# Four blocks of a cross-attention kernel made one, its high parts taken straight from the exponent, and its output computed in 512-token units

## The chip, the cores and the metric

The kernel runs on one core of a Trainium2 chip. The metric is the device time of one execution in microseconds (us), the median of a few runs. A core has five engines that work side by side, each through its own list of instructions in order: TensorE (PE, matrix products into the accumulator memory PSUM; its weight loads are listed as PEld), VectorE (DVE), ScalarE (ACT), GpSimd (POOL) and SyncE (SP, which here only issues DMA transfers). They wait for one another through counting semaphores.

## The reference

Two batches of 1024 query tokens with 640 features attend to 2044 context tokens with 384 features, in 8 heads of 80 (`D`). The four context tokens behind those form a second, small attention: they ask over the residual, and the result asks four keys again. Both results are summed, multiplied by `Wout`, and bias and residual are added. Cut to what matters:

```
query = hidden_states @ Wq;  keyt = enc @ Wk;  valt = enc @ Wv      # enc: 2044 tokens
hs = mha(query, keyt, valt)                                         # 8 heads of 80
ca_q1 = einsum('btc,th->bch', ca, Wq_ca)[:, indices, :]             # ca: 4 tokens
ca_hs1 = mha(ca_q1, residual, residual)
ca_hs2 = mha(ca_hs1 @ Wq, ca @ Wk_ca, ca @ Wv_ca)
out = (hs + ca_hs2) @ Wout + b_out + residual
```

## The kernel before

All arithmetic is float32. TensorE runs the large products in its faster `fp32r` format, in which an operand has fewer bits, so each operand is split into a high part (the value rounded to `fp32r`) and a low part (value minus high part), and a product is three matmuls: high by high, high by low, low by high. ScalarE makes high parts, VectorE low parts.

The program is four blocks, one after another. At the end of a block (`with nc.Block()`) all engines meet at a barrier before any of them begins the next.

- **project** (0 to about 291 us). For both batches, 512 tokens at a time, it makes keys, values, queries and `u` (for the small attention) in a fixed list of `jobs`. Job n writes PSUM bank n % 8; ScalarE evicts the high part, VectorE the low part, and SP writes both to HBM. Interleaved "m" jobs find score maxima of the small attention. `ctx_f` holds two context chunks as they arrive. At the first job of chunk c ScalarE splits chunk c+1 (`split_ctx`, L403), also at the very first job of all.
- **tokens** (to about 456 us): the small attention, 16 heads of four steps. `scores` (L942), ACT's exponent (L770), products with the residual (L973); in between `fold_tokens` (L897) and `fold_keys` (L906) combine weights; `gather` (L926) and `low_gathered` (L839) make `p2g` at the end, `fold_values` (L917) makes `vw`. SP begins with `written`, a wait until all of project's writes have landed, then loads `wk2`, `wqT` (L717) and later the first head's keys. Before that, in project, eight small DMAs (`shift_tokens`, L633) put negated maxima in place; a head's scores wait for all eight.
- **attend** (to about 1178 us): the main attention, 16 heads (`G`) of 16 key tiles (`KT`), so 256 steps `n`. A step is: scores of tile n+2 (four matmuls, L1166) into one of two PSUM tiles `at_s_ps`; ACT's exponent of it to `probs` (L1107), and a second ACT pass over `probs` that makes the high part `prob_hi` (L1113); the low part `prob_lo` on VectorE (L1041), or for tiles 4, 9 and 14 of a head on GpSimd; and six matmuls of tile n's values (L1183). Two further matmuls per step (`score_piece`, L177) compute scores of the next head so that VectorE (L185) can take their maxima; the last head has no such pieces. The score PSUM tile is free after L1107. The values wait for the low part ahead of all six matmuls. After a head ACT takes the result (L1119), and SP, VectorE and GpSimd (L222) divide it by the sum and write it to `heads_d`.
- **output** (the rest): 16 tiles of 128 tokens. Each loads its `heads_d` piece (L1252), the residual (L1254) and a piece of `p2g` (L1255), splits it (ACT L1281, DVE L1304), runs 30 + 2 matmuls (L1335, L1339) into one of two PSUM tiles, adds residual and bias (L1318) and stores. The last head's division runs beside the first tiles.

A group of matmuls is paced by what its weights and moving operand cost and by the semaphores in front of it. What sets the order of the work around the change is only the order in which the code is written, engine by engine, and these waits.

## Time and profile before

| | |
|---|---|
| three runs | 1273.33, 1271.99, 1273.00 us; median 1273.0 |
| the profiled execution | 1273.22 us, its span 1271.4 us |
| PE busy | 1234.0 us, 97% of the span |
| DVE, ACT, POOL busy | 820.8 (65%), 721.3 (57%), 209.6 us (16%) |
| largest idle times in front of a matmul | 7.0 us (start of output), 5.2 (start of tokens), 4.4 (in project), 3.1 us (start of attend) |

The span is the time from the first to the last instruction of the profiled execution; the 1.8 us around it are not in the trace. The engines' shares are averages over stages with different limits. The ends of matmuls in the timeline are modelled and overlap the next start, so the pace of a run of matmuls is read from start to start. The granted clock of PE is given as a share of 2.4 GHz: 1.00 is 2.4 GHz, 0.50 is 1.2 GHz. In a timeline, what stands in brackets is the time for which the engine did nothing before the row, and what ended it.

### The profile page before, as it was taken

The numbers are of one execution on the slowest core, as the hardware profiler recorded it, in microseconds if no ns is written. First come the engines' busy times: TensorE is split into PE (matmuls) and PEld (weight loads), VectorE is DVE, ScalarE is ACT, GpSimd is POOL, SyncE is SP. The second block draws the span as 40 slices with busy tenths as digits, with TensorE's granted clock in tenths as the row PEclk, the third lists the DMA queues.
The fourth block names the chain that finished last, engine by engine and source line by source line (L and its number), as shares of the span: only waits on it lengthen the run. The fifth ranks groups of instructions, "written<-read, shape, count | busy, mean of one in ns | idle before, by whom it ended". The sixth has DMA issues, their size and how long they took to land. (4 is left out here: it accounts for less than half of the span.)

```text
span 1271.4 us, 15103 instructions
## 1 busy us (share of the span) xinstructions
PE 1234.0 (97%) x5652; PEld 968.8 (76%) x5652; DVE 820.8 (65%) x1147; ACT 721.3 (57%) x784; POOL 209.6 (16%) x112
## 2 busy tenths in 40 slices
PE   6999999998999989999999999999999999999798
PEld 5888988896667667777777777777777777776798
DVE  4448825681234368888888888888887887864223
ACT  5332424222444456777777777777777777778111
POOL 1100000000000011212212321221221222123232
PEclk9999999997999999999999999999999999999899
DMA  7995798896650052453254244335425424210566
GB/s 245 281 334 193 208 288 238 276 260 142 191 147 1 1 153 78 112 141 95 77 146 104 82 127 110 107 107 146 97 71 146 104 89 120 65 53 22 166 201 185
DMA packets 106686, 181.44 MB, mean 143 GB/s; under 512 B 18185, under 2 KB 62729, under 8 KB 102490
## 3 DMA queue, kind: packets, MB, share of 16 engines
q1 hardware_dynamic: 101194, 162.71, 46.7%
q0 software_dynamic: 2688, 11.80, 2.9%
q10 hardware_dynamic: 2736, 6.03, 1.3%
q8 instruction: 42, 0.69, 0.2%
q14 instruction: 26, 0.21, 0.1%
HBM read 116.32 MB, written 63.24 MB: 141 GB/s over the span
## 5 line engine op out<-in xcount | busy, mean ns | idle before, releaser
L185 DVE TENSOR_REDUCE mpart<-at_mx_ps 128x1 f32<-128x512 f32 x480 | 326.2, 685 | 108.5 <-PE at_mx_ps L177 106.4
L1107 ACT ACTIVATE probs<-at_s_ps 128x1024 f32<-128x1024 f32 (+1 forms) x256 | 262.7, 1026 | 158.1 <-PE at_s_ps L1166 158.1
L1041 DVE TENSOR_TENSOR prob_lo<-probs,prob_hi 128x1024 fp32r<-128x1024 f32 (+1 forms) x208 | 270.3, 1299 | 38.0 <-ACT prob_hi L1113 37.9
L1113 ACT ACTIVATE prob_hi<-probs 128x1024 fp32r<-128x1024 f32 (+1 forms) x256 | 271.4, 1060 | 7.6
L1041 POOL TENSOR_TENSOR prob_lo<-probs,prob_hi 128x1024 fp32r<-128x1024 f32 x48 | 115.3, 2403 | 551.8 <-ACT prob_hi L1113 551.8
L177 PE MATMUL at_mx_ps<-ka,qa 128*128 128x512 f32 x480 | 196.4, 409 | 0.0
L177 PEld LDWEIGHTS at_mx_ps<-ka,qa 128*128 128x128 f32 x480 | 153.7, 320 | 34.2 <-DVE mpart L185 4.4
L1166 PE MATMUL at_s_ps<-qa,ka 128*128 128x512 f32 (+1 forms) x512 | 162.3, 398 | 3.1 <-PEq L706 3.1
L1183 PE MATMUL at_o_ps<-prob_hi,v_hi 128*81 128x512 f32 (+1 forms) x512 | 162.6, 399 | 2.1 <-POOL prob_lo L1041 1.0
L1166 PE MATMUL at_s_ps<-qb,kb 113*128 113x512 f32 (+1 forms) x512 | 161.1, 396 | 0.0
L1183 PE MATMUL at_o_ps<-prob_lo,v_hi 128*81 128x512 f32 (+1 forms) x512 | 160.1, 394 | 0.0
L1183 PE MATMUL at_o_ps<-prob_hi,v_lo 128*81 128x512 f32 (+1 forms) x512 | 159.9, 393 | 0.0
L1166 PEld LDWEIGHTS at_s_ps<-qa,ka 128*128 128x128 f32 (+1 forms) x512 | 96.7, 189 | 35.9 <-issue 3.6
L1166 PEld LDWEIGHTS at_s_ps<-qb,kb 113*128 113x128 f32 (+1 forms) x512 | 99.2, 194 | 12.4
L1183 PEld LDWEIGHTS at_o_ps<-prob_lo,v_hi 128*81 128x81 f32 (+1 forms) x512 | 76.1, 149 | 41.7
L1183 PEld LDWEIGHTS at_o_ps<-prob_hi,v_hi 128*81 128x81 f32 (+1 forms) x512 | 74.8, 150 | 40.2 <-issue 7.1
L464 ACT ACTIVATE out_hi<-bank 128x512 fp32r<-128x512 f32 x60 | 35.3, 598 | 107.3 <-PE bank L617 98.9
L1183 PEld LDWEIGHTS at_o_ps<-prob_hi,v_lo 128*81 128x81 f32 (+1 forms) x512 | 78.3, 153 | 22.5
L546 DVE TENSOR_TENSOR out_lo<-bank,out_hi 128x512 fp32r<-128x512 f32 x60 | 40.7, 688 | 59.3 <-ACT out_hi L464 59.1
L1335 PE MATMUL o_ps<-wq_store,o_hs_hi 128*128 128x320 f32 x320 | 63.0, 320 | 9.8 <-DVE o_hs_lo L1304 9.8
L770 ACT ACTIVATE p<-s_ps 128x768 f32<-128x768 f32 x42 | 33.9, 809 | 57.2 <-PE s_ps L942 57.2
L617 PE MATMUL bank<-wv_hi,ctx_hi 128*128 128x320 f32 x192 | 60.5, 315 | 4.4 <-DVE out_lo L546 4.4
(131 smaller groups left out, 1566.3 us busy)
## 6 DMA issues: line engine op xcount, KB each, us to landing
v_hi_d<-v_t SPq DMA_DIRECT2D x16, 648.0 KB, 9.3
v_lo_d<-v_t SPq DMA_DIRECT2D x16, 648.0 KB, 11.8
v_hi<-v_hi_d SPq DMA_DIRECT2D x16, 648.0 KB, 4.7
v_lo<-v_lo_d SPq DMA_DIRECT2D x16, 648.0 KB, 5.9
k_hi_d<-out_hi SPq DMA_DIRECT2D x40, 256.0 KB, 4.9
k_lo_d<-out_lo SPq DMA_DIRECT2D x40, 256.0 KB, 6.1
ka<-k_hi_d SPq DMA_DIRECT2D x16, 640.0 KB, 7.5
kb<-k_hi_d SPq DMA_DIRECT2D x16, 640.0 KB, 11.1
```

Source lines behind the costliest of these rows:

```text
L177: pe.matmul(self.mx_ps[k % 2][:, 0:w], self.qa[g % NA][:, qt:SQ:ST], self.ka[g % NA][:, c * CH:c * CH + w], start=True, stop=True).then_in ...
L185: dve.tensor_reduce(self.mpart[:, g % 2, qt, c:c + 1], self.mx_ps[k % 2][:, 0:w], AX, ALU.max).then_inc(self.mx_done, 1)
L464: act.activation(ring[nr % RING][0][:], banks[n % 8][:], ACT.Copy).then_inc(hi_done, 1)
L546: dve.tensor_tensor(lo[:], bank[:], hi[:].bitcast(F32), ALU.subtract).then_inc(done, 1)
L617: mm = pe.matmul(to, a, y, start=k == 0 and i == 0, stop=k == nk - 1 and i == 2)
L770: act.activation(p1[k % 3][:], s_ps[k % 2][:, :, 0:CD], ACT.Exp, scale=SCALE).then_inc(e_done, 1)
L1041: eng.tensor_tensor(pl[n % PB][0:r, :], prob[n % PF][0:r, :], ph[n % PB][0:r, :].bitcast(F32), ALU.subtract).then_inc(sem, 1)
L1107: act.activation(prob[n % PF][0:r, :], s_ps[n % 2][0:r, :], ACT.Exp, scale=SCALE).then_inc(e_done, 1)
L1113: act.activation(ph[n % PB][0:r, :], prob[n % PF][0:r, :], ACT.Copy).then_inc(ph_done, 1)
L1166: mm = pe.matmul(s_ps[n % 2][0:r, u * CH:(u + 1) * CH], a[0:rows, t * P:t * P + r], y[0:rows, u * CH:(u + 1) * CH], start=first, stop=not ...
L1183: mm = pe.matmul(o_ps[:, u * CH:(u + 1) * CH], a[0:r, t, :], y[n % PB][0:r, u * CH:(u + 1) * CH], start=t == 0 and m == 0, stop=t == KT - ...
L1335: pe.matmul(ps[p][:, u, 0:HALF], a[:, m, :], y[:, m, u * HALF:(u + 1) * HALF], start=m == 0 and k == 0, stop=False)
```

## The change

1. **One block.** The four blocks become one, in which each engine runs its part of all four stages in order. Where a barrier kept PSUM banks and buffers apart there are now waits: `evicted` lets the first token scores start when their own banks have been emptied, `folded_values` and `gathered` do the same for the main attention, and `written` waits for project's matmuls too. `shift_tokens` of batch 1 is shared between SP and POOL, with one semaphore for each head.
2. **First chunk split.** `split_ctx(0, 1)` moves from the first key job to the first query job.
3. **Two exponents.** ACT computes the exponent twice from PSUM: first to `prob_hi`, then to `probs`. Hence the score tile is free after the second. The values wait for the high part first, and for the low part only ahead of their last two matmuls. The low parts of the last two tiles are always VectorE's.
4. **Output.** The head results are no longer loaded tile by tile: four units of 512 tokens (2 for each batch, 1280 KB each) are loaded into buffers of the attention that are free by then. Units 0 and 1 (batch 0) are loaded during the last two heads and split by VectorE in the last head, step 1 to 10, one fifth of a unit a step (`high_part`, a copy to `fp32r`, and `low_part`). Units 2 and 3 are loaded when the last head is written; ACT splits them between tiles. Four PSUM tiles instead of two, three result buffers, residual tiles loaded by ACT's queue, `p2g` read where it lies, loops unrolled.

Key, query and value buffers are also joined in pairs (`ka`, `qa` become `a`; `kb`, `qb` become `b`; `v_hi`, `v_lo` become `v`), so that a unit fits; what is computed with them is the same. The diff, without re-indentation and renaming (the first piece stands so in ACT's and in DVE's part):

```diff
     for n, (kind, c, m) in enumerate(jobs):
-        if kind == "k" and m == 0 and c < NS - 1:
+        if kind == "k" and m == 0 and c < NS - 1 and (b or c):
             split_ctx(b, c + 1)
+        if (b, kind, c, m) == (0, "q", 0, 0):
+            split_ctx(0, 1)
...
-                            shift_tokens(sp, kept, ca, b)
+                        shift_tokens(sp, kept, ca, b, range(0, NH, 2))
+            pool.wait_ge(top_done, 2 * B)
+            shift_tokens(pool, kept, ca, B - 1, range(1, NH, 2))
...
         def written(eng):
+            eng.wait_ge(full, (B + 1) * NJ)
+        def evicted(pe, left):
+            pe.wait_ge(done, B * NJ + 8 - left)
...
-                    if k % (NH * pairs) == 0:
-                        pe.wait_ge(ntop_in[b], 16 * NH)
+                if j == 0:
+                    pe.wait_ge(ntop_in[b][h], 16)
-                    if k >= 2:
+                if k < 2:
+                    evicted(pe, 4 - 2 * k)
+                else:
                         pe.wait_ge(e_done, k - 1)
...
-        on_pool = [n % KT in POOL_T for n in range(N)]
+        on_pool = [n % KT in POOL_T and n < N - 2 for n in range(N)]
         def make_low(eng, n, sem):
-            eng.wait_ge(ph_done, n + 1)
+            eng.wait_ge(e_done, n + 1)
...
                     act.wait_ge(s_full, n + 1)
+                if n >= PB:
+                    act.wait_ge(pv_done, n + 1 - PB)
+                act.activation(ph[n % PB][0:r, :], s_ps[n % 2][0:r, :], ACT.Exp, scale=SCALE
+                               ).then_inc(ph_done, 1)
+                between()
                     if n >= PF:
                         wait_low(act, n - PF)
                     act.activation(prob[n % PF][0:r, :], s_ps[n % 2][0:r, :], ACT.Exp, scale=SCALE
                                    ).then_inc(e_done, 1)
-                    between()
-                    act.wait_ge(e_done, n + 1)
-                    if n >= PB:
-                        act.wait_ge(pv_done, n + 1 - PB)
-                    act.activation(ph[n % PB][0:r, :], prob[n % PF][0:r, :], ACT.Copy).then_inc(ph_done, 1)
...
-                    wait_low(pe, n)
+                pe.wait_ge(ph_done, n + 1)
                     for m, (a, y) in enumerate(((hi, ph), (lo, ph), (hi, pl))):
+                    if y is pl:
+                        wait_low(pe, n)
...
-                for n in range(2):
-                    scores(n, lambda: None)
+            folded_values(pe)
+            scores(0, lambda: None)
+            gathered(pe, 1)
+            scores(1, lambda: None)
+            gathered(pe, B)
...
+        def high_part(dve, i, m):
+            if m == 0:
+                dve.wait_ge(hs_in[i], 16)
+            dve.tensor_copy(high[i][:, m], whole[i][:, m].bitcast(F32)).then_inc(hi[i], 1)
+        def low_part(dve, i, m):
+            dve.wait_ge(hi[i], m + 1)
+            dve.tensor_tensor(whole[i][:, m], whole[i][:, m].bitcast(F32), high[i][:, m].bitcast(F32),
+                              ALU.subtract).then_inc(lo[i], 1)
+        def early_split(dve, t):
+            if t == 1:
+                dve.wait_ge(at.s_full, (G - 1) * KT)
+            if t == 6:
+                dve.wait_ge(at.pv_done, (G - 1) * KT)
+            if 1 <= t < 1 + 2 * MC:
+                i, m = divmod(t - 1, MC)
+                high_part(dve, i, m)
+                low_part(dve, i, m)
+        def sync(sp):
+            at.spread(sp, scratch, G - 1)
+            at.put(sp, scratch, G - 1)
+                for p in range(2):
+                sp.wait_ge(at.hs_out[p], 16 * G // 2)
+            sp.wait_ge(at.s_full, N)
+            load_unit(sp, 2)
+            sp.wait_ge(at.pv_done, N)
+            load_unit(sp, 3)
```

In the order of instructions, the first place is ACT in project, around the first evictions. Before:

```order
L411 ACTIVATE x_hi<-x_f 128x2560 [waits pj_full,pj_x0_in]
L403 ACTIVATE ctx_hi<-ctx_f 128x1536 [waits pj_full,pj_ctx_in1]
L464 ACTIVATE out_hi<-bank 128x512 [waits pj_ring_out0,pj_full]
L464 ACTIVATE out_hi<-bank 128x512 [waits pj_ring_out1,pj_full]
L464 ACTIVATE out_hi<-bank 128x512 [waits pj_ring_out2,pj_full]
```

And now:

```order
L436 ACTIVATE x_hi<-x_f 128x2560 [waits pj_full,pj_x0_in]
L491 ACTIVATE out_hi<-bank 128x512 [waits pj_ring_out0,pj_full]
L491 ACTIVATE out_hi<-bank 128x512 [waits pj_ring_out1,pj_full]
L491 ACTIVATE out_hi<-bank 128x512 [waits pj_ring_out2,pj_full]
L491 ACTIVATE out_hi<-bank 128x512 [waits pj_ring_out3,pj_full]
L491 ACTIVATE out_hi<-bank 128x512 [waits pj_ring_out4,pj_full]
L451 ACTIVATE wq_store<-ca_f 128x3200 [waits pj_w_in3]
L483 ACTIVATE v_t<-bank 128x4x80 [waits pj_w_lo,pj_wk_lo,pj_full]
L483 ACTIVATE v_t<-bank 128x4x80 [waits pj_full] x7
L428 ACTIVATE ctx_hi<-ctx_f 128x1536 [waits pj_full,pj_ctx_in1]
```

The split of the second chunk, which waits for its load (`pj_ctx_in1`), has moved behind five key and eight value evictions.

The second place is PE in the main attention, one step. Before (`at_exp` is the exponent, `at_pl_dve` the low part):

```order
L1166 MATMUL at_s_ps<-qa,ka 128x512 [waits at_exp]
L1166 MATMUL at_s_ps<-qa,ka 128x512
L177 MATMUL at_mx_ps<-ka,qa 128x512 [waits at_mx_done]
L1166 MATMUL at_s_ps<-qb,kb 128x512 x2
L1183 MATMUL at_o_ps<-prob_hi,v_hi 81x512 [waits at_pl_dve]
L1183 MATMUL at_o_ps<-prob_hi,v_hi 81x512
L177 MATMUL at_mx_ps<-ka,qa 128x508 [waits at_mx_done]
L1183 MATMUL at_o_ps<-prob_hi,v_lo 81x512 x2
L1183 MATMUL at_o_ps<-prob_lo,v_hi 81x512 x2
```

And now (`at_exp` is the second exponent, `at_ph` the first):

```order
L1204 MATMUL at_ps<-a 128x512 [waits at_exp]
L1204 MATMUL at_ps<-a 128x512
L204 MATMUL at_ps<-a 128x512 [waits at_mx_done]
L1204 MATMUL at_ps<-b 128x512 x2
L1223 MATMUL at_ps<-prob_hi,v 81x512 [waits at_ph]
L1223 MATMUL at_ps<-prob_hi,v 81x512
L204 MATMUL at_ps<-a 128x508 [waits at_mx_done]
L1223 MATMUL at_ps<-prob_hi,v 81x512 x2
L1223 MATMUL at_ps<-prob_lo,v 81x512 [waits at_pl_dve]
L1223 MATMUL at_ps<-prob_lo,v 81x512
```

The matmuls are the same twelve; the wait for the low part has moved back past four value matmuls and a piece, and a wait for the high part stands in its old place.

The third place is DVE in the last head. Before, with the last head's sixteen low parts but those on POOL:

```order
L1041 TENSOR_TENSOR prob_lo<-probs,prob_hi 124x1024 [waits at_ph]
L1041 TENSOR_TENSOR prob_lo<-probs,prob_hi 128x1024 [waits at_ph] x4
L201 RECIPROCAL rden<-den 128x8 [waits at_den_in0]
L1041 TENSOR_TENSOR prob_lo<-probs,prob_hi 128x1024 [waits at_ph] x8
L1041 TENSOR_TENSOR prob_lo<-probs,prob_hi 124x1024 [waits at_ph]
```

And now, from the same place as far as the third step's split (steps up to 10 go on like this):

```order
L1082 TENSOR_TENSOR prob_lo<-probs,prob_hi 124x1024 [waits at_exp]
L1082 TENSOR_TENSOR prob_lo<-probs,prob_hi 128x1024 [waits at_exp] x3
L1306 CAST a<-a 128x512 [waits o_hs_in0,at_s_full]
L1310 TENSOR_TENSOR a<-a 128x512 [waits o_hi0]
L1082 TENSOR_TENSOR prob_lo<-probs,prob_hi 128x1024 [waits at_exp]
L1306 CAST a<-a 128x512
L1310 TENSOR_TENSOR a<-a 128x512 [waits o_hi0]
L228 RECIPROCAL rden<-den 128x8 [waits at_den_in0]
L1306 CAST a<-a 128x512
L1310 TENSOR_TENSOR a<-a 128x512 [waits o_hi0]
```

Behind the low part of every step stand a copy (CAST) and a subtraction of 512 columns that were not there.

## Rows read from the trace of the kernel before

**Rows 1.** The page: span; busy us, share and instructions of each engine

```profile
span 1271.4 us, 15103 instructions
...
PE 1234.0 (97%) x5652; PEld 968.8 (76%) x5652; DVE 820.8 (65%) x1147; ACT 721.3 (57%) x784; POOL 209.6 (16%) x112
```

**Rows 2.** Windows: PE, PEld, DVE, ACT, POOL busy, granted clock, DMA share

```profile
28.00:30.00 2.00, 1.27 (x5) 1.27 (x6) 2.00 (x5) 2.00 (x3) 0.00 (x0) 0.50 0.39 150
```

**Rows 3.** Timeline, first 80 us: start, duration, engine, instruction, [idle before]

```profile
24.80 1.48 ACT L403 ACTIVATE ctx_hi<-ctx_f 128x1536 fp32r<-128x1536 f32 x1 [6.91 <-DMA ctx_f<-in_ctxT]
...
28.73 0.64 PE L617 MATMUL bank<-wv_hi,ctx_hi 128*128 128x320 f32 x1 [4.42 <-DVE out_lo L546]
...
33.43 0.34 PE L617 MATMUL bank<-wv_hi,ctx_lo 128*128 128x320 f32 x1
...
75.06 0.60 ACT L464 ACTIVATE out_hi<-bank 128x512 fp32r<-128x512 f32 x1 [3.59 <-DMA q_lo_d<-out_lo]
```

**Rows 4.** Timeline where the projections end and the token attention begins

```profile
295.46 1.62 PE L942 MATMUL s_ps<-ca,u 97*128 97x384 f32 x4 [5.15 <-PEq L307]
...
305.06 0.39 SPq L717 DMA_DIRECT2D wqT<-in_wqT  x1
...
318.08 5.88 PE L906 MATMUL f_ps<-bd,wqT 128*80 128x64 f32 x80
```

**Rows 5.** DMA issues, 280 to 330 us: count, KB each, us to landing

```profile
wqT<-in_wqT SPq DMA_DIRECT2D x1, 1600.0 KB, 10.7
```

**Rows 6.** Timeline where the token attention ends and the main one begins

```profile
454.57 1.22 DVE L839 TENSOR_TENSOR p2g<-s_ps,p2g 32x1024 fp32r<-32x1024 f32 x1 [1.83 <-ACT p2g L761]
...
456.59 1.07 PE L1166 MATMUL at_s_ps<-qa,ka 128*128 128x512 f32 x2 [3.11 <-PEq L706]
...
463.74 0.63 PE L1166 MATMUL at_s_ps<-qa,ka 128*128 128x512 f32 x2
```

**Rows 7.** By line, 480 to 1100 us: count, busy us, mean ns, idle before

```profile
L1113 ACT ACTIVATE prob_hi<-probs 128x1024 fp32r<-128x1024 f32 x218 | 231.1, 1060 | 6.5
...
L1107 ACT ACTIVATE probs<-at_s_ps 128x1024 f32<-128x1024 f32 x219 | 224.8, 1026 | 138.7 <-PE at_s_ps L1166 138.7
```

**Rows 8.** Timeline at the end of the attention and the start of the output

```profile
1163.54 3.42 POOL L222 TENSOR_TENSOR x_hi_place<-x_hi_place,x_f 80x1024 f32<-80x1024 f32 x1
...
1165.78 2.27 DVE L1041 TENSOR_TENSOR prob_lo<-probs,prob_hi 128x1024 fp32r<-128x1024 f32 x1 [1.10 <-ACT prob_hi L1113]
...
1175.51 0.70 PE L1183 MATMUL at_o_ps<-prob_hi,v_hi 128*81 128x512 f32 x2 [1.01 <-POOL prob_lo L1041]
...
1177.89 0.63 PE L1183 MATMUL at_o_ps<-prob_lo,v_hi 124*81 124x512 f32 x2
...
1185.49 1.44 PE L1335 MATMUL o_ps<-wq_store,o_hs_hi 128*128 128x320 f32 x4 [6.97 <-DVE o_hs_lo L1304]
```

**Rows 9.** The chain that ended last: start us, us, what

```profile
1207.29 4.40 PE o_ps L1335 x30
...
1211.69 0.30 PE o_ps L1339 x2
...
1228.71 5.94 PE o_ps L1335 x30
...
1267.88 0.82 DVE o_o L1318
```

**Rows 10.** DMA issues of 1178 to 1272 us

```profile
heads_d<-x_f SPq DMA_DIRECT2D x1, 320.0 KB, 3.9
...
x_f<-rden_d SPq DMA_DIRECT2D x1, 320.0 KB, 3.2
...
den<-x_f SPq DMA_DIRECT2D x1, 4.0 KB, 4.5
```

**Rows 11.** DMA issues of 30 to 110 us

```profile
x_f<-in_xT POOLq DMA_DIRECT2D x2, 1280.0 KB, 10.5
```

**Rows 12.** Timeline of DVE, first 20 us

```profile
6.42 0.69 DVE L496 TENSOR_TENSOR ctx_lo<-ctx_f,ctx_hi 128x512 fp32r<-128x512 f32 x1 [6.42 <-ACT ctx_hi L420]
```

1710 lines of the change are left out of this document (870 added, 840 removed).

## The prediction

> **What bounds the kernel now.** I read the page first: TensorE is busy 97% of 1271.4 us [rows 1], so at most some 37 us of it is idle, and no other engine has more than 65%. Then the list of waits for PE, the busy time by windows for its granted clock, and the timelines around each idle stretch. The idle time is in few places: in project 4.4 us [rows 3], at the barrier ahead of tokens 5.2 us [rows 4], at the barrier ahead of attend 3.1 us [rows 6], in the last step of attend 1.0 and ahead of the output 7.0 us [rows 8], and inside the output ahead of the tile at 1228.7 [rows 9]. After an idle stretch the clock is at its 1.2 GHz level for a while: 0.50 at 28 to 30 us [rows 2]. Between these places PE never stops, so only what it computes and these places count. The change leaves PE's matmuls as they are; each term is an idle stretch taken away.
>
> **Start of project.** ACT waits 6.9 us for the second chunk and splits it until 26.3 before it evicts the first keys; PE, out of banks, stands 4.4 us until 28.73 [rows 3]. Now the first evictions come ahead of that split. PE then runs at half clock to 33.43: eighteen 320-column matmuls in 4.70 us, at 0.147 each (4.40 / 30, rows 9) worth 2.64, a loss of 2.1. Together 6.5. What is late next: the DMA engines. At 75.06 ACT evicts a key only when the write out of its ring buffer has landed [rows 3]; PE needs that bank again about 1.5 us after it is free, which is all the slack. The writes begin earlier by as much as PE, into a stretch with DMA share 0.39 [rows 2], so I take 6.0; ends: 2.0 (only 1.5 plus a little is kept) and 6.6.
>
> **Projections to tokens.** PE stands 5.2 us until 295.46 [rows 4] although the first head's maxima are there; then the first four score matmuls take 1.62 us at half clock and the first step is about 1.2 us longer than the later ones. With a semaphore for each head and the PSUM waits, PE starts at about 290.3, and is ready for `fold_keys` 6.6 us sooner, at 311.5 instead of 318.08. But `wqT` is issued at 305.06, after the wait for all written values, and lands in 10.7 us, at 315.8 [rows 4, 5]. Its cover was the barrier; now it ends last. SP issues four of the eight small DMAs instead of eight, some 2.8 us less in front of the value writes, so it lands at 313.0 or so. Gain 318.1 - 313.0 = 5.1. Ends: 2.3 (the load is not earlier) and 6.6 (it is no wait at all). POOL's four small DMAs stand in an empty POOL queue.
>
> **Tokens to attend.** Before, scores start at 456.59 and the scores of tile 3 at 463.74 [rows 6]. Now the first scores start when tokens' last matmul is through (453.5) and the second right behind. `gathered(2)` holds PE until VectorE's 454.57 + 1.22 = 455.8 [rows 6]; the exponents of tile 0 run from 454.7 to 456.7 (2 x 1.03, rows 7), so tile 2's scores start at 456.8, tile 3's when tile 1's second exponent is done, 458.8, and PE is there at 459.1: 4.6 sooner. VectorE, with up to three maxima and a low part a step, keeps back some of it in the first twelve steps; I take 4.3 (3.0 to 4.9).
>
> **Main loop.** ACT does as much as before: 1.026 + 1.060 us a step becomes twice 1.026 [rows 7]. The score tile is released by the second pass instead of the first, about 1.03 us later. ACT waits 138.7 us in 219 steps for PE's scores, 0.63 us a step [rows 7]: it is early, and the release is still over half a us ahead of the scores that want it even where `take` stands between the passes. The added wait of each step: in an output tile the two matmuls behind a wait take 0.30 us, against 2 x 0.147 [rows 9], so 0.007 us a wait, 256 x 0.007 = 1.8 us. Ends 0 and 2.6. I take a loss of 1.8.
>
> **Last head.** VectorE gets ten copies and ten subtractions of 512 columns. A subtraction is 0.69 [rows 12]. No such copy is in the trace; as one input is less to read it is bounded by 0.69 above and, by half the columns it could at best be worth, 0.35 below. VectorE's step is then 1.22 + 0.69 + 0.35 to 0.69 = 2.3 to 2.6 us against PE's ten matmuls, 2.33. Over ten steps, two low parts of which are POOL's, that is 20 to 24 us against 23. VectorE and POOL also hold each other up: the POOL multiply at 1163.54 runs for 3.42 us, until 1166.96, and the VectorE subtraction at 1165.78 beside it takes 2.27 instead of the 1.22 of the same 1024 columns at 454.57 [rows 6], and ends 1.09 us after POOL does [rows 8]. A low part may be about 2 us late now, since four value matmuls go ahead of it. I take a loss of 0.8 us, ends 0 and 5.
> The Trainium skill ("SBUF — State Buffer", Who interferes with whom) says that VectorE and GpSimd lock a shared pair of ports for a whole instruction, and that a copy in a two-port mode takes that lock too. The two rows at 1163 and 1165 agree with a lock, to 0.1 us. "VectorE: DVE Perf Modes" (Mode 2×_2P) gives such a copy twice the rate; no row here shows it. By the one rule the loss would be nearer its upper end, by the other nearer its lower.
>
> **End of attend and output.** Before: PE waits 1.0 us for POOL's low part, starts again at 1175.51 and issues its last pair at 1177.89; with the low part on VectorE and later in the step it should issue it at 1176.7, 1.2 sooner. The output starts at 1185.49 [rows 8] and the span ends at 1271.4. After: tile 0 needs only what was split in the last head, and starts 0.46 us behind the last pair, at 1177.2. A tile is 4.40 + 0.30 = 4.70 [rows 9], sixteen are 75.2: 1252.4. The tail is unchanged: the last subtraction starts at 1267.88 before, its tiles' last matmul starting 0.3 earlier, and the span ends 3.5 us later; that gives 1252.4 + 0.3 + 3.5 = 1256.2. Gain 15.2.
> Does unit 2 come in time for tile 8, at 1177.2 + 37.6 = 1214.8? ACT's take ends at 1178.4; then `den` 4.5, reciprocal 0.2, `rden` no more than 4.5 again, broadcast 3.2, multiply 3.4, write 3.9 [rows 8, 10]: 1198.1. The unit is 1280 KB, as a load that took 10.5 us among others [rows 11]: 1208.6. ACT's pass of 2560 columns is 2.5 x 1.06 = 2.7, VectorE's five subtractions 3.5: 1214.8. So even the sum of the longest is just in time; with transfers in a quiet queue I expect some 5 to 8 us to spare. The stall is nothing, at most 4.
>
> **Sum.** 6.0 + 5.1 + 4.3 - 1.8 - 0.8 + 15.2 = 28.0. The profiled execution took 1273.2 (1271.4 and 1.8 around it) and is 0.2 above the median of the runs, 1273.0. So 1273.0 - 28.0 = 1245.0.
>
> **Rivals.**
> - *The per-buffer waits stop PE where the barriers did* (16%). For: `wqT` ends last already in my own working, project's writes are near the DMA engines' limit. Then the first three terms give their low ends, 2.0 + 2.3 + 3.0 = 7.3 instead of 15.4: 1253. Against: the maxima, banks and exponents are ready in the rows.
> - *The last head's VectorE or unit 2 becomes the bound* (10%). Copy at 0.69 and each POOL operation blocking: 5 instead of 0.8, and the unit 4 late: 8.2 more, 1253.
> - *More than I count* (9%). All upper ends and no cost of the wait: 6.6 + 6.6 + 4.9 + 15.2 = 33.3: 1240, or below if PE's seams between heads shrink.
> - *Slower: the score tile comes free too late* (3%). The mechanism is the second exponent in front of `at_exp`, in every step. A step has two buffers; if the release, 1.03 us later, were behind PE's wish by more than 28 / 256 = 0.11 us a step, nothing is left. If ACT's 0.63 us of waiting were the whole slack, PE would lose 0.4 us a step, 102 us: 1347. Against: the scores of tile n+2 are wanted only after values, scores and values of other tiles; 0.63 is ACT's idle time, not the slack.
>
> **How the numbers follow.** My forecast, 1245 with its own range of 1241 to 1250, has 62%, the rivals 38%. Two of them lie at 1253; the range 1238 to 1254 leaves out the slow case and the tails. A measurement of this kernel cannot tell changes under 0.2% (2.5 us) from none. All cases but the last are faster by far more: faster 0.96, same 0.01, slower 0.03.
>
> **What would show it.** In the profile after: PE without a gap at 24 to 29 us and the second chunk's split behind the value evictions; the first token scores within 1 us of the last value matmul, and `fold_keys` at about 306 to 307 after a short wait for `wqT`; no idle over 1 us where the main attention begins; steps at the old pace; in the last head a VectorE copy between 0.35 and 0.69; the output's matmuls one block of 75 us right behind the attention, tile 8 without a wait. It is wrong if PE's pace in the main loop moves by over 0.5%, if PE waits for low parts in the last head, or if idle time reappears in front of a DMA.

## The result, and the profile after

The changed kernel takes 1244.56 us in the median of four runs (1242.70 to 1245.66) against 1272.55 for the one before; the ratio is 0.9778 with a 95% interval of 0.9761 to 0.9795. The forecast was 1245.0. Its total was right, but two of its terms were off by 4.6 and 4.8 us in opposite directions, and that these cancelled is luck. What follows is mostly about these two.

The profiled execution was the fastest of the four (1242.70 us), so the two traces lie 30.5 us apart (spans of 1271.4 and 1240.9), the medians 28.0. The page of the changed kernel, its rows as in [rows 1]:

```profile
span 1240.9 us, 14533 instructions
...
PE 1222.9 (99%) x5652; PEld 963.0 (78%) x5652; DVE 832.9 (67%) x1162; ACT 678.5 (55%) x770; POOL 209.8 (17%) x115
```

The list of waits for PE (what waited, for whom: us in total, times, longest):

```profile
PE bank L591 <- ACT wk_hi L447: 7.1, 1, 7.1
PE at_ps L1223 <- DVE prob_lo L1082: 4.2, 1, 4.2
```

Apart from the wait for the first weights, all the idle stretches of before of over 1.0 us are gone, and there is a new one: 4.2 us for a low part of VectorE. To see what each stage is worth, I read the same landmarks in both traces: the first value matmul, the last one, the first matmul of `fold_keys`, and ScalarE's taking of each head's result. First the timeline of PE, SyncE and, for the landing, the DMA list:

```profile
19.13 0.30 PE L644 MATMUL bank<-wv_hi,ctx_hi 128*128 128x320 f32 x1
...
282.42 0.31 PE L644 MATMUL bank<-wv_hi,ctx_lo 128*128 128x320 f32 x1
282.56 0.86 PE L967 MATMUL s_ps<-ca,u 97*128 97x384 f32 x4
...
290.26 3.41 PE L920 MATMUL f_ps<-x_f 128*128 128x8 f32 x30
293.53 6.04 PE L920 MATMUL f_ps<-x_f,x_hi_place 128*128 128x8 f32 x30
...
293.67 0.39 SPq L746 DMA_DIRECT2D wqT<-in_wqT  x1
...
305.16 5.02 PE L929 MATMUL f_ps<-bd,wqT 128*80 128x64 f32 x68
...
wqT<-in_wqT SPq DMA_DIRECT2D x1, 1600.0 KB, 10.4
```

The first score matmuls of the tokens follow the last value matmul at once (before: 5.2 us of idle time, [rows 4]). Now ScalarE's takes of heads 0, 13, 14 and 15, before and after:

```profile
508.65 1.02 ACT L1119 ACTIVATE x_hi_place<-at_o_ps 81x1024 f32<-81x1024 f32 x1 [0.60 <-PE at_o_ps L1183]
1097.43 1.02 ACT L1119 ACTIVATE x_f<-at_o_ps 81x1024 f32<-81x1024 f32 x1 [0.61 <-PE at_o_ps L1183]
1141.15 1.02 ACT L1119 ACTIVATE x_hi_place<-at_o_ps 81x1024 f32<-81x1024 f32 x1 [0.38 <-PE at_o_ps L1183]
1178.56 1.02 ACT L1119 ACTIVATE x_f<-at_o_ps 81x1024 f32<-81x1024 f32 x1 [3.30 <-PE at_o_ps L1183]
```

```profile
491.07 1.02 ACT L1157 ACTIVATE x_hi_place<-at_ps 81x1024 f32<-81x1024 f32 x1 [0.60 <-PE at_ps L1223]
1077.44 1.02 ACT L1157 ACTIVATE x_f<-at_ps 81x1024 f32<-81x1024 f32 x1 [0.61 <-PE at_ps L1223]
1120.62 1.02 ACT L1157 ACTIVATE x_hi_place<-at_ps 81x1024 f32<-81x1024 f32 x1 [0.36 <-PE at_ps L1223]
1162.22 1.02 ACT L1157 ACTIVATE x_f<-at_ps 81x1024 f32<-81x1024 f32 x1 [2.24 <-PE at_ps L1223]
```

Between takes 0 and 13 a head takes 45.29 us before and 45.11 after. The last head takes 37.41 before and 41.60 after. The table sets the landmarks against the forecast; in the traces before, the last value matmul starts at 290.01, and the first one at 20.20.

| stretch (us) | before | after | gain | forecast |
|---|---|---|---|---|
| start to last value matmul | 290.01 | 282.42 | 7.6 | 6.0 |
| to `fold_keys` | 28.07 | 22.74 | 5.3 | 5.1 |
| to take 0 | 190.57 | 185.91 | 4.7 | 4.3 |
| take 0 to take 14 | 632.50 | 629.55 | +3.0 | -1.8 |
| take 14 to take 15 | 37.41 | 41.60 | -4.2 | +0.4 |
| take 15 to the span's end | 92.84 | 78.68 | 14.2 | 14.0 |
| sum | | | 30.5 | 28.0 |

(Of the forecast's 15.2 for the end, 1.2 lies ahead of take 15; with the -0.8 that is the +0.4.) The output is what the forecast said: in the chain that ended last it is one block of sixteen tiles, the first at 1162.18 and the last at 1232.68, so (1232.68 - 1162.18) / 15 = 4.70 us each.

```profile
1162.18 4.41 PE at_ps L1396 x30
...
1232.68 4.42 PE at_ps L1396 x30
```

The last head is not. Here are VectorE, GpSimd and PE around the 4.2 us (start, duration; in brackets the idle time ahead):

```profile
1139.83 0.42 DVE L1306 CAST v<-b 128x512 fp32r<-128x512 f32 x1
1140.28 2.87 DVE L1310 TENSOR_TENSOR b<-b,v 128x512 fp32r<-128x512 f32 x1
1143.07 2.65 DVE L1306 CAST v<-b 128x512 fp32r<-128x512 f32 x1
...
1147.59 2.55 DVE L1082 TENSOR_TENSOR prob_lo<-probs,prob_hi 128x1024 fp32r<-128x1024 f32 x1
...
1140.20 2.40 POOL L1082 TENSOR_TENSOR prob_lo<-probs,prob_hi 128x1024 fp32r<-128x1024 f32 x1 [9.03 <-ACT probs L1150]
1142.56 2.88 POOL L249 TENSOR_TENSOR x_hi_place<-x_hi_place,x_f 80x1024 f32<-80x1024 f32 x1
1145.52 3.54 POOL L1337 TENSOR_TENSOR u_place<-u_place 128x640 f32<-128x640 f32 x2
...
1150.19 0.69 PE L1223 MATMUL at_ps<-prob_lo,v 128*81 128x512 f32 x2 [4.19 <-DVE prob_lo L1082]
```

A copy of 512 columns takes 0.42 us, a subtraction 0.69, a low part 1.22; together with their overlap VectorE needs 2.20 us for a step of 2.33. It has no lack of time of its own. But from 1140.20 to 1149.06 GpSimd works without a break (a low part, the multiply of head 14, two additions of residual and bias), and the operations of VectorE beside it take 2 to 6 times as long. Each ends soon after a GpSimd operation: the subtraction at 1143.15, 0.55 behind 1142.60; the low part at 1150.14, 1.08 behind 1149.06. That is about what it would need if it had begun only when GpSimd's had ended (0.14 us less than it takes alone, in both). GpSimd's operations are longer too: the multiply takes 2.88 us here and 2.40 in head 2 (at 561.56, below). PE has the low part 4.19 us late, and its next matmuls run at half clock, which costs another 1.8 us (6.0 in all against late_split, below).

### The profile page after: what moved, and what is told of

Read it like the earlier page. It is cut to its first block, busy times and chain, and to the rows that moved or that the text cites. A ratio compares the mean times of both kernels' runs of the same rounds, so it can differ in the third digit from the quotient of the medians.

```text
span 1240.9 us, 14533 instructions
## 1 busy us (share of the span) xinstructions
PE 1222.9 (99%) x5652; PEld 963.0 (78%) x5652; DVE 832.9 (67%) x1162; ACT 678.5 (55%) x770; POOL 209.8 (17%) x115
## 4 chain that ended last, share of the span: by engine, by line
PE 96%; DVE 2%; ACT 1%; issue 1%; DMA 0%; ACTq 0%
PE at_ps L1223 28%; PE bank L644 19%; PE at_ps L1204 18%; PE at_ps L204 9%; PE acc_t_ps L1000 7%; PE at_ps L1396 6%; PE s_ps L967 2%; PE bank L621 2%; PE bank L591 1%; PE f_ps L940 1%; PE acc_t_ps L978 1%; PE f_ps L920 1%; DVE prob_lo L1082 1%; PE f_ps L204 1%; PE f_ps L929 0%
## 5 line engine op out<-in xcount | busy, mean ns | idle before, releaser
L212 DVE TENSOR_REDUCE mpart<-at_ps 128x1 f32<-128x512 f32 x480 | 326.5, 686 | 109.4 <-PE at_ps L204 107.8
L1145 ACT ACTIVATE prob_hi<-at_ps 128x1024 fp32r<-128x1024 f32 (+1 forms) x256 | 263.2, 1028 | 199.2 <-PE at_ps L1204 199.2
L1223 PE MATMUL at_ps<-prob_hi,v 128*81 128x512 f32 (+1 forms) x1024 | 319.7, 397 | 0.2 <-issue 0.2
L1150 ACT ACTIVATE probs<-at_ps 128x1024 f32<-128x1024 f32 (+1 forms) x256 | 261.0, 1019 | 0.0
L1223 PEld LDWEIGHTS at_ps<-prob_hi,v 128*81 128x81 f32 (+1 forms) x1024 | 154.0, 152 | 59.5 <-issue 6.6
L204 PE MATMUL at_ps<-a 128*128 128x512 f32 x480 | 194.2, 405 | 0.5 <-DVE p2g L865 0.5
L204 PEld LDWEIGHTS at_ps<-a 128*128 128x128 f32 x480 | 153.7, 320 | 32.7 <-DVE mpart L212 1.3
L1223 PE MATMUL at_ps<-prob_lo,v 128*81 128x512 f32 (+1 forms) x512 | 160.0, 394 | 4.2 <-DVE prob_lo L1082 4.2
L1204 PE MATMUL at_ps<-a 128*128 128x512 f32 (+1 forms) x512 | 161.8, 397 | 0.0
L1204 PE MATMUL at_ps<-b 113*128 113x512 f32 (+1 forms) x512 | 160.7, 395 | 0.0
```

What stands on the lines that cost most here:

```text
L204: pe.matmul(mx_ps[k % 2][:, 0:w], self.queries_a(g)[:, qt:SQ:ST], self.keys_a(g)[:, c * CH:c * CH + w], start=True, stop=True).then_inc(se ...
L212: dve.tensor_reduce(self.mpart[:, g % 2, qt, c:c + 1], mx_ps[k % 2][:, 0:w], AX, ALU.max).then_inc(self.mx_done, 1)
L1145: act.activation(ph[n % PB][0:r, :], s_ps[n % 2][0:r, :], ACT.Exp, scale=SCALE).then_inc(ph_done, 1)
L1150: act.activation(prob[n % PF][0:r, :], s_ps[n % 2][0:r, :], ACT.Exp, scale=SCALE).then_inc(e_done, 1)
L1204: mm = pe.matmul(s_ps[n % 2][0:r, u * CH:(u + 1) * CH], a[0:rows, t * P:t * P + r], y[0:rows, u * CH:(u + 1) * CH], start=first, stop=not ...
L1223: mm = pe.matmul(o_ps[:, u * CH:(u + 1) * CH], a[0:r, t, :], y[n % PB][0:r, u * CH:(u + 1) * CH], start=t == 0 and m == 0, stop=t == KT - ...
```

## The experiments

Twelve runs, each beside runs of the kernel before on the same chip. They are on three chips, on which the kernel before takes 1273.04, 1273.79 and 1272.79 us. All edits are to the changed kernel. Differences of 2 to 6 us are near what medians of four runs can tell (the changed kernel's own runs span 3 us), so the profile of each carries the argument, landmark by landmark.

### One cause at a time, up to the main attention

**split_first** puts the second chunk's split back.

```diff
-                    if kind == "k" and m == 0 and c < NS - 1 and (b or c):
+                    if kind == "k" and m == 0 and c < NS - 1:
                         split_ctx(b, c + 1)
-                    if (b, kind, c, m) == (0, "q", 0, 0):
-                        split_ctx(0, 1)
```

> The changed kernel with only the split of the second context chunk put back ahead of the first key evictions. Theory A (the idle time and the half clock behind it are what the move saved): PE stands about 4.4 us from 24.3 us on and then runs some 4.7 us at half clock; all later work comes 6.5 us later, and nothing is given back at the writes around 60 to 70 us; time 1251 us. Theory B (the 7.6 us by which project's end came earlier is all due to the move): 7.6 us later, 1252 us, and the first value matmul starts at the same time in both. Theory A has it that 1.07 of the 7.6 is the time at which the clock comes up in the first key matmuls, which differs from run to run.

Measured 1249.63 us. From the first value matmul (20.05) to the last (289.91) it is 269.86 us, against 263.29 with the move: the move is worth 6.57, theory A. (The time is 1.4 us under the 1251 of that theory: in the profiled execution the half clock behind `fold_tokens` is the short one, below.) The idle stretch is back:

```profile
28.74 0.64 PE L640 MATMUL bank<-wv_hi,ctx_hi 128*128 128x320 f32 x1 [4.58 <-DVE out_lo L570]
```

The remaining 1.0 of the 7.6 lies ahead of the first value matmul, which in all fourteen profiles starts anywhere from 18.57 to 20.27 us, whatever the kernel.

**block_pt** and **block_ta** put a barrier back: two `nc.Block()` instead of one, behind project or behind tokens. **block_unshared** is block_pt with all eight small DMAs of batch 1 on SyncE.

```diff
+        with nc.Block() as block:      # project alone
+            ...
         with nc.Block() as block:
-                projecting.tensor(pe)
                 asking.tensor(pe)
                 attending.tensor(pe)
                 ending.tensor(pe)
# block_unshared besides:
-                        shift_tokens(sp, kept, ca, b, range(0, NH, 2))
+                        shift_tokens(sp, kept, ca, b, range(NH))
-            pool.wait_ge(top_done, 2 * B)
-            shift_tokens(pool, kept, ca, B - 1, range(1, NH, 2))
```

> The changed kernel with a barrier between the projections and the token attention, as before. Theory A (as the two traces say): PE stands 5.1 to 5.2 us, the first scores run at half clock, the half clock behind the small folding matmuls is 1.6 us cheaper; fold_keys comes 5.3 us later and the time is 1249 us. Theory B (the load of wqT was what ended last): fold_keys is 5.3 later too, but PE waits for the load in front of it in this kernel or in the changed one.

> The changed kernel with a barrier behind the projections and all eight small DMAs of the maxima issued by SyncE, as before both. With the barrier alone PE stood 2.6 us. Theory A (the barrier waits for SyncE's last issue, and SyncE is 2.6 us behind with four more small DMAs in its queue): PE stands 5.2 us, fold_keys comes 2.6 us later than with the barrier alone, time 1249. Theory B (the barrier alone makes the stand, and its 2.6 us was a matter of the run): as with the barrier alone, 1246 to 1247.

Measured 1246.21 us and 1251.68; 1249 was expected of both. My expectation for block_pt failed: PE stands 2.6 us, not 5.2. The row of block_pt and of block_unshared, and ahead of each SyncE's last issue of the stage:

```profile
284.33 0.58 SPq L416 DMA_DIRECT2D v_lo_d<-v_t  x1
...
285.50 0.94 PE L967 MATMUL s_ps<-ca,u 97*128 97x384 f32 x4 [2.61 <-PEq L1472]
```

```profile
284.40 2.58 SPq L414 DMA_DIRECT2D v_lo_d<-v_t  x1
...
287.57 1.62 PE L965 MATMUL s_ps<-ca,u 97*128 97x384 f32 x4 [4.60 <-PEq L1470]
```

The barrier waits for SyncE to be through its list. The last issue begins at the same time in both, but behind eight small DMAs it takes 2.58 us and not 0.58, so it holds SyncE until 286.98 instead of 284.91. PE starts 0.59 us behind its end in both, and in before 0.60 us behind the end of SyncE's last issue (292.00 to 294.86; PE starts at 295.46).

The cost is read up to the start of `fold_tokens`, since behind it the clock differs from run to run. From the last value matmul to that point it is 7.84 us in the changed kernel, 12.20 in block_pt, 14.85 in block_unshared and 14.81 in before. So the barrier with the half clock behind it costs 4.4 us, and that it stood behind eight small DMAs another 2.6, together the 7.0 of before. Of these, 1.64 come back behind `fold_tokens`, where the clock of before stays down for less (below), and that leaves the 5.3 of the table. Sharing the DMAs would have gained the 2.6 with the barrier in place. Up to `fold_keys` block_pt takes 25.47 us instead of 22.74 and block_unshared 31.39: the first has the short half clock, the second the longest.

> The changed kernel with a barrier between the token attention and the main one. Theory A: PE stands 3.1 us and runs at half clock for 3.5 us, first head result 4.7 us later, time 1248 to 1249 us, and no step after the first head changes. Theory B (the wait for VectorE's maxima in the first steps gives part of it back): 3 us later or less.

Measured 1247.81 us. PE stands 2.89 us; from `fold_keys` to take 0 it is 189.44 instead of 185.91, so 3.5 of the 4.7 is the barrier. one_exponent below gives another 0.3 (186.20). The last 0.8 was not separated.

**fold_halves** splits `fold_tokens` in two.

```diff
-                if k == 3:
-                    fold_tokens()
+                if k in (2, 3):
+                    fold_tokens(k - 2)
```

> The changed kernel with the 60 small matmuls of fold_tokens (8 columns each) in two halves of 30, one behind step 2 and one behind step 3 of the token attention. They run 3.4 us at full clock, but in the changed kernel the clock falls to half 3.8 us after they begin and stays there for 10.5 us, some 5 us lost. Theory A (one long run of them brings the clock down): the clock stays up, PE is ready for fold_keys about 5 us sooner, and then stands 3 to 4 us for wqT, which lands 10.4 us after its issue and has only 1 us to spare now; gain 1 us, time 1242 to 1243. Theory B (any such matmuls bring it down): clock as before, no change, 1244. Theory C: the clock stays up and the load is no bound: 5 us faster, 1239.

Measured 1245.62 us: nothing gained. The clock still falls, twice, for about 3.5 us each; `fold_keys` comes 21.28 us behind the last value matmul, 1.5 sooner, and the weight load that needs `wqT` now waits 0.6 us for it. But split_first and one_exponent, with all 60 matmuls in one run, have 21.11 and 21.12 where their half clock was short. The gain does not stand out of the spread of the runs.

This stretch has something of its own. The matmuls of `fold_tokens` have 8 columns, and in the changed kernel the clock falls to 1.2 GHz soon behind their start, with PE busy all the time (a window: length, busy of PE, PEld, DVE, ACT, POOL, granted clock, DMA share, GB/s; the clock was 1.00 from 292 to 294 us and 0.53 from 294 to 296):

```profile
296.00:298.00 2.00, 2.00 (x11) 2.00 (x11) 0.00 (x0) 0.00 (x0) 0.00 (x0) 0.50 1.01 367
```

From the start of `fold_tokens` to that of `fold_keys` it is 13.26 us in before, and 13.26, 13.27 or 13.27 in three of the variants; 14.89 to 14.93 in both profiles of the changed kernel and in four others; 16.54 in block_unshared: steps of 1.64 us by how long the clock stays down. (bias_early has 14.25, with 0.83 of it a wait for `wqT`; fold_halves and best_spread have other work in between.)

### The main loop

**one_exponent** goes back to one exponent and a copy, **low_first** to the old place of the wait for the low part.

```diff
# one_exponent
-                act.activation(ph[n % PB][0:r, :], s_ps[n % 2][0:r, :], ACT.Exp, scale=SCALE
-                               ).then_inc(ph_done, 1)
                 act.activation(prob[n % PF][0:r, :], s_ps[n % 2][0:r, :], ACT.Exp, scale=SCALE
                                ).then_inc(e_done, 1)
+                between()
+                act.activation(ph[n % PB][0:r, :], prob[n % PF][0:r, :], ACT.Copy).then_inc(ph_done, 1)
# low_first
+                wait_low(pe, n)
                 pe.wait_ge(ph_done, n + 1)
                 for m, (a, y) in enumerate(((hi, ph), (lo, ph), (hi, pl))):
-                    if y is pl:
-                        wait_low(pe, n)
```

> The changed kernel with one exponent and a second pass that copies it to the high part, as before; the new place of the wait for the low part stays. Theory A (the two exponents' second pass ends 0.14 us earlier than exponent and copy did, so GpSimd starts its low part earlier in the step, and VectorE, which is held until GpSimd's operation ends, comes back sooner): the head period goes from 45.10 back to 45.29 us, PE's stand in the eleventh step of each head from 0.09 to 0.25 us, 2.5 us over the run; time 1247. Theory B (the period came from the later wait for the low part): period stays 45.10, time 1244 to 1245. In both the stand in the last head stays.

> The changed kernel with PE's wait for the low part back ahead of all six value matmuls, two exponents kept. Theory A: the head period stays 45.10 us (the extra wait behind the fourth matmul costs nothing), the last head's stand begins four matmuls earlier and is 0.9 us longer, 5.1 instead of 4.2, and the first step of the main attention is later by up to 1 us; time 1245 to 1247. Theory B (the extra wait costs 0.007 us in each step, as I forecast): 1.8 us less in the main loop, period 44.99. Theory C (the wait's place made the period): period 45.29.

Measured 1247.56 us and 1243.46. The head period is 45.290 in one_exponent, within 0.001 of before (45.291) although the added wait is still there, and 45.115 in low_first against 45.105, not the 44.99 that a wait of 0.007 us would give: the second exponent alone makes it, and the place of the wait and the wait itself cost nothing. From take 0 to take 14 one_exponent takes 632.14 us, so the second exponent gives 2.6 of the 3.0 us; the other 0.4 lies in head 14 and was not separated. Where the 0.19 us of each head comes from shows in the step in which GpSimd multiplies the head before. In the changed kernel, and then in one_exponent:

```profile
562.92 2.12 DVE L1082 TENSOR_TENSOR prob_lo<-probs,prob_hi 128x1024 fp32r<-128x1024 f32 x1
...
561.56 2.40 POOL L249 TENSOR_TENSOR x_f<-x_f 80x1024 f32<-80x1024 f32 x1
```

```profile
562.91 2.30 DVE L1082 TENSOR_TENSOR prob_lo<-probs,prob_hi 128x1024 fp32r<-128x1024 f32 x1
...
561.73 2.40 POOL L249 TENSOR_TENSOR x_f<-x_f 80x1024 f32<-80x1024 f32 x1
```

VectorE starts its low part at the same time in both and is held until GpSimd's multiply ends, at 563.96 or 564.13; it ends 1.08 us behind that in both. GpSimd is 0.17 earlier in the changed kernel since its own low part, ahead of the multiply, waits for ScalarE's second pass, and the two exponents start 0.92 us apart (565.57, 566.49), exponent and copy 1.06 (583.37, 584.43 before). PE's score pieces want their bank back from VectorE, and PE is held up that much less: level until 565.37 and 565.36, it begins the scores of the next step at 567.09 in the changed kernel and at 567.27 in one_exponent. That it is the bank is read from the order of the rows; no row names the wait. In the last head of low_first PE stands in three places (3.1, 0.5 and 0.3 us, and not once for 5.1 as I expected), with more half clock behind them: from take 13 to take 15 it is 86.32 us instead of 84.78. That its median lies 1.0 below the changed kernel's, on another chip, is within the spread of both.

### The last head

**bias_early** moves GpSimd's first two additions to the end of head 14. **late_split** has VectorE split units 0 and 1 behind the last low part. **best** is bias_early with tile 9 on VectorE and unit 1's pieces elsewhere, **best_spread** adds `fold_tokens` in four parts. **after_again** is the changed kernel once more.

```diff
# bias_early, best: attend's gpsimd
+                if (g, t) == (G - 2, 14):
+                    early_bias(pool)
# late_split: early_split does nothing, and in output's vector
+            for i in range(2):
+                for m in range(MC):
+                    high_part(dve, i, m)
+                    low_part(dve, i, m)
             at.invert(dve, G - 1)
# best
-        on_pool = [n % KT in POOL_T and n < N - 2 for n in range(N)]
+        on_pool = [n % KT in POOL_T and n < N - 8 for n in range(N)]
-            if 1 <= t < 1 + 2 * MC:
+            if 1 <= t <= MC or 9 <= t < 12:
# best, in output's vector
+            for m in range(3, MC):
+                high_part(dve, 1, m)
+                low_part(dve, 1, m)
             at.invert(dve, G - 1)
# best_spread
-                if k == 3:
-                    fold_tokens()
+                if k < 4:
+                    fold_tokens(k)
```

> The changed kernel with GpSimd's two additions of residual and bias for the first two output tiles moved from the middle of the last head to the end of the head before it. VectorE's own work in the last head is the same. Theory A (a VectorE subtraction or copy that meets a GpSimd operation is held until that operation ends): with GpSimd busy until 1145.4 instead of 1149.1, VectorE has the low part for step 12 ready at about 1147.5 instead of 1150.1; PE stands 1.7 instead of 4.2 us and the half clock behind it (1.7 us) goes or shrinks: 2.5 to 4.2 us faster, 1241. Theory B (VectorE simply has 2.33 us of work for a step of 2.33 us): the stand is as long as now, no gain, 1244.

Measured 1238.87 us (ratio to before 0.9726, 0.9710 to 0.9743). VectorE's work in the head is what it was, and only GpSimd's two additions have gone; PE stands 1.63 us:

```profile
1146.84 1.22 DVE L1082 TENSOR_TENSOR prob_lo<-probs,prob_hi 128x1024 fp32r<-128x1024 f32 x1
...
1148.12 0.68 PE L1225 MATMUL at_ps<-prob_lo,v 128*81 128x512 f32 x2 [1.63 <-DVE prob_lo L1082]
```

Take 13 to take 15 is 80.61 us instead of 84.78, so 4.2 less with the half clock. That is theory A's number (2.5 to 4.2); theory B would have left it alone. The time is 2 us under the 1241 that was expected. The profiled execution is 3.7 us shorter than that of the changed kernel, so the stretch accounts for the profiles; for the rest of the difference nothing is shown.

> The changed kernel without the splits in the last head: VectorE splits units 0 and 1 behind the last low part. The last head loses nothing any more (stand of 4.2 us and 1.9 us at half clock gone: take 13 to take 15 78.7 us), but output tile 0 waits for unit 0's five copies and subtractions of 1.11 us each, from 1155.1 on: PE stands 4.6 us and has half clock after it, 1.5 to 3 us. Theory A (the splits in the last head nearly pay only for themselves, because of the stand): time within 2 us of the changed kernel, 1243 to 1246. Theory B (they are worth their full 7 us of idle time): 1250.

> The changed kernel once more, beside the others. 1244.6, with the same stands of PE: 4.2 us in the last head and none over 1 us elsewhere behind the first matmul. By theory A of the runs before, its executions differ by how long the first matmuls run at half pace (first value matmul at 18.6 to 20.3 us) and by 1.64 us in the stretch behind fold_tokens.

Measured 1244.34 us and, for the changed kernel, 1244.45. Without the splits take 13 to take 15 is 78.76 us, 6.0 less, and PE pays it back in front of output tile 0:

```profile
1161.19 6.58 PE L1393 MATMUL at_ps<-wq_store,a 128*128 128x320 f32 x30 [4.47 <-DVE a L1310]
```

With the half clock behind this wait, take 15 to the span's end is 86.24 us instead of 78.68, so 7.6 more. As it was placed, splitting two units in the last head saved 7.6 us ahead of the output and cost 6.0 in the head: 1.5 us are left between the two profiles, and the medians (runs of 1243.66 to 1246.36 and 1242.37 to 1245.85) do not show even that. Of the 6.0, 4.2 went in bias_early, where only two of GpSimd's operations were moved. In late_split VectorE's low parts are held beside GpSimd too (four from 1145.29 take 8.44 us), but without copies and subtractions between them it has time to spare, and PE does not wait.

> The changed kernel with bias_early's edit, the low part of tile 9 of the last head on VectorE instead of GpSimd, and unit 1's five pieces at other places: three at steps 9 to 11 of the last head, two behind its last low part, where VectorE stands 4.1 us. GpSimd's multiply then falls beside steps 5 to 7, which carry no piece. If VectorE is late only where it meets GpSimd's operations (theory A): no stand of PE over 0.3 us in the last head, from take 13 to take 15 78.9 us instead of 84.8, end 6 us earlier than the changed kernel and 1.7 before bias_early: 1237 to 1238. Theory B (VectorE has too much work in the last head, now 1.2 us more of it): a stand of 1 us or more stays and the time is that of bias_early or worse, 1239 or more.

> The kernel best with fold_tokens in four parts, one behind each of the first four steps of the token attention. Theory A (only a long run of such matmuls lowers the clock): the clock stays up, 5 us of half clock go, but PE then stands for wqT, about 3.5 to 4 us, and the gain is 0.5 (short case of the half clock) to 1 us or more (long case, by 1.64 us): 1236. The time varies less from run to run. Theory B (the parts still bring the clock down): no gain, 1237.5.

Measured 1238.02 us for best (ratio 0.9722, 0.9709 to 0.9736), 6.4 below the changed kernel on the same chip. Theory A's limit of 0.3 us was missed: one stand of 1.05 is left, and by the same cause, since the multiply now falls beside the piece of step 5:

```profile
1133.73 2.95 DVE L1312 TENSOR_TENSOR a<-a 128x512 fp32r<-128x512 f32 x1
...
1133.71 2.42 POOL L249 TENSOR_TENSOR x_hi_place<-x_hi_place,x_f 80x1024 f32<-80x1024 f32 x1 [2.50 <-DMA x_f<-rden_d]
...
1137.87 0.69 PE L1225 MATMUL at_ps<-prob_lo,v 128*81 128x512 f32 x2 [1.05 <-DVE prob_lo L1082]
```

With the stand smaller than bias_early's by 0.6 its median is 0.85 lower, on a chip on which before is 1.0 lower as well; the two are not told apart. best_spread took 1239.39 us. Its profile shows the steps of theory A: the clock stays at 1.00, PE is ready 4.7 us sooner (301.26, and 283.42 for the first scores, against 305.13 and 282.54 in best), and stands for the load of `wqT`:

```profile
296.00:298.00 2.00, 2.00 (x18) 2.00 (x19) 0.08 (x1) 0.00 (x0) 0.00 (x0) 1.00 0.99 364
...
304.38 5.80 PE L930 MATMUL f_ps<-bd,wqT 128*80 128x64 f32 x78 [3.12 <-DMA wqT<-in_wqT]
```

But its time was to be 1236 and to vary less, and neither came true: its runs lie from 1236.95 to 1240.72 (those of best from 1237.12 to 1238.87) and are not faster than best. The profiled one was among the two fastest (1237.33). These two have a mean granted clock of 1.000, the three longer ones 0.997 to 0.999, and 0.003 of 1240 us is 3.7 us, about the 3.8 between the ends. So the clock probably fell somewhere in the longer ones; where, no trace shows.

## Why the prediction was right, and where it was not

- **Start of project** (6.0). The working was 6.5, measured 6.57. I took off 0.5 since the DMA engines might keep back PE. In the profile of the changed kernel they hardly do: one matmul, at 68.83 us, starts 0.33 us behind the one before it, and those around it 0.147 apart. But the mechanism is real. In five of the thirteen profiles with the changed kernel or a variant, PE waits 0.15 to 0.82 us at this place. In block_unshared, whose edits all lie later, ScalarE evicts a bank only when a query write has landed, VectorE makes the low part until 69.01 us, and PE has stood for the bank:

```profile
67.69 0.60 ACT L489 ACTIVATE out_hi<-bank 128x512 fp32r<-128x512 f32 x1 [2.27 <-DMA q_lo_d<-out_lo]
...
69.07 0.42 PE L642 MATMUL bank<-wv_hi,ctx_hi 128*128 128x320 f32 x1 [0.82 <-DVE out_lo L572]
```

From the first value matmul to the last it is 264.09 us there. The other 1.1 us of the 7.6 is how long the first matmuls run at half pace, which differs from run to run; it is no effect of the change.
- **Projections to tokens** (5.1; measured 5.3). The size was right and the path partly wrong. `wqT` did not end last in the profiled execution: it landed at 304.1 and PE came at 305.16. PE had gained 7.0 us up to `fold_tokens`, and lost 1.64 to a half clock that stayed longer than before's, a term that the forecast does not have. Where the half clock was short, the load and PE come almost together: in split_first and one_exponent it had landed by 0.0 to 0.2 us, and in bias_early PE waited 0.8 us for it; without the half clock (best_spread) it waited 3.1. So the forecast's next bound is real, and just behind the one that counted. What I had not seen is that 2.6 of the 7.0 us was SyncE's eight DMAs in front of the barrier.
- **Tokens to attend** (4.3; 4.7). Right, within the ends of 3.0 to 4.9. VectorE's `gathered` keeps PE 0.5 us.
- **Main loop** (-1.8; +3.0). The step that failed is the price of the added wait, 0.007 us in 256 steps. I took it from an output tile whose last two matmuls also change operands, and its own lower end, 0, was right: one_exponent, which keeps the wait, has the period of before. And I took "ACT does as much as before" for no effect. ScalarE's second pass ends 0.17 us sooner, GpSimd's low part and multiply with it, and VectorE, held behind the multiply, comes back sooner in each head.
- **Last head** (-0.8 and +1.2; -4.2). The mechanism stood in the forecast: VectorE and GpSimd hold each other up. I read it in [rows 8] and priced it as rare, by adding the copies to VectorE's work and comparing sums over ten steps. This is the step that failed, the 0.8. By late_split the splits cost 6.0 us, 4.2 of them a stand and 1.8 the half clock behind it, and that is above my upper end of 5. The +1.2 was 1.8 (37.41 us from take 14 to take 15 before, 35.62 in late_split), which took back a part. The copy's price was right (0.42 in 0.35 to 0.69). The fault is that the new operations also turn GpSimd operations of the head into waits, and that GpSimd's last four come in one run of 8.9 us.
The Trainium skill says this ("SBUF — State Buffer", Who interferes with whom): when a VectorE copy in a two-port mode and a GpSimd instruction meet, the one that issues first has the shared ports for the whole instruction and the other blocks fully; a VectorE instruction with two inputs in SBUF contends with a GpSimd instruction that reads SBUF; a reduction never does. The traces agree: copy 2.65 for 0.42, subtraction 2.87 for 0.69. The maximum beside GpSimd's low part of 559.20 keeps its 0.69, though it reads PSUM, so that this does not tell a reduction from its place of input. "VectorE: DVE Perf Modes" of the Trainium skill (Mode 2×_2P), on the copy at twice the rate, agrees too: subtractions of 512 and 1024 columns take 0.69 and 1.22, so 0.53 for 512 columns and 0.16 fixed (an estimate from these rows), and half of 0.53 with the 0.16 is 0.43, against 0.42 measured.

```profile
559.20 2.41 POOL L1082 TENSOR_TENSOR prob_lo<-probs,prob_hi 128x1024 fp32r<-128x1024 f32 x1 [10.05 <-ACT probs L1150]
...
559.52 0.69 DVE L212 TENSOR_REDUCE mpart<-at_ps 128x1 f32<-128x512 f32 x1 [0.38 <-PE at_ps L204]
```

- **Output** (14.0 of 15.2; 14.2). Right to 0.2. Unit 2 was split at 1196.8, 3 us ahead of tile 8 (1199.78), where I had expected 5 to 8. The unit itself landed early, 6.9 us behind its issue at 1176.57. But ScalarE splits it only behind the store of tile 4, and tile 4 waited until 1188.19 for its residual and bias. Its residual was issued at 1177.55, right behind the two units of 1280 KB, and landed 8.9 us later, where the median of these loads is 3.9; the DMA share is 0.98 to 1.05 from 1180 to 1188 us. So the transfers did take the time to spare, through the small load beside them.

```profile
1177.55 0.57 ACTq L1290 DMA_DIRECT2D u_place<-in_x  x1
...
1186.54 1.56 POOL L1337 TENSOR_TENSOR u_place<-u_place 128x640 f32<-128x640 f32 x1 [7.80 <-DMA u_place<-in_x]
...
1188.19 0.82 DVE L1369 TENSOR_TENSOR probs<-at_ps,u_place 128x640 f32<-128x640 f32 x1 [6.36 <-POOL u_place L1337]
...
1189.98 2.34 ACT L1357 ACTIVATE b<-a 128x2560 fp32r<-128x2560 f32 x1 [26.74 <-DVE probs L1369]
1192.39 4.45 DVE L1310 TENSOR_TENSOR a<-a,b 128x512 fp32r<-128x512 f32 x5
```

The rivals: of the second, the last head came true, with 5.2 us more than forecast where it had 4.2 (4.6 with the better end), and the late unit did not. The main loop's 4.8 went the way of the third (more than I count), though no part of it names their cause. That the two cancelled is luck: the sum would have been 5 us off with either alone. The slow case, the score tile freed too late, showed nothing: PE never waits for an exponent in the main loop.

## What to carry to other kernels

When work is put on VectorE beside GpSimd, do not add up durations; list GpSimd's operations in that stretch and count, for each, one wait of its full length for the copy or the subtraction that meets it, and ask whether several stand in a row. A barrier costs what the slowest list in front of it costs, and a queue that only issues DMAs can be that list. A large load can be in time itself and still make a small one beside it late. A total that comes out right says little about its terms; read the same landmarks in both traces before trusting them.

## What the runs showed of the chip that I had not expected

- PE can be busy without a gap and still fall to 1.2 GHz: matmuls of 8 columns (60 in 9.2 us in the changed kernel) were followed by it in every profile but best_spread's, where the same ones stand in runs of 12 to 18 with wider ones between. Two runs of 30 (fold_halves) still did it. One profile without the fall is little, and that the narrow matmuls are the cause is not shown further.
- The first matmuls of the program run at half pace while the clock column says 1.00. Five of 512 columns have 2.47 us at 7.08 and 1.29 at 12.33. How long that lasts differs between executions: in block_unshared the full pace is there by 10.63, in before by 13.37. Below, two rows of the timeline and the window in between.

```profile
7.08 2.47 PE L591 MATMUL bank<-ctx_hi,wk_hi 128*128 128x512 f32 x5 [7.08 <-ACT wk_hi L447]
...
12.33 1.29 PE L591 MATMUL bank<-ctx_hi,wk_hi 128*128 128x512 f32 x5
...
8.00:10.00 2.00, 2.00 (x6) 1.53 (x5) 1.72 (x3) 1.52 (x3) 0.00 (x0) 1.00 1.04 411
```

- Two exponents from PSUM start 0.92 us apart, an exponent and a copy of its result 1.06, on the same 1024 columns.
